# Decoder layer on one core: row normalisations and two bias-free evictions on ScalarE, the maximum's PSUM banks shared, every engine's list reordered

## The reference

```
x = _layernorm(x + attn(x))             # 16 heads of 16, biases, rotary with the row's norm, layernorm of q and k heads, causal
x = _layernorm(x + xattn(x, ctx))       # over the 256 columns: 8 heads of 8, band of 64, relu(o @ w_out.T + b_out) * ctx, w_ct, b_ct
x = _layernorm(x + ffn(x))              # ternary quantised weights, silu(gate) * up (1024 wide), rms_norm, projection

def _layernorm(x, axis=-1, eps=1e-05):
    m = jnp.mean(x, axis=axis, keepdims=True)
    v = jnp.var(x, axis=axis, keepdims=True)
    return (x - m) / jnp.sqrt(v + eps)
```

## Time and profile before

| what | value |
|---|---|
| median of 3 runs | 1081.5 us (1079.98 to 1083.27) |
| the profiled execution's own time | 1079.87 us |
| its span, first to last instruction | 1078.1 us |
| DVE busy | 944.7 us, 88% of the span |
| PE busy | 933.3 us, 87% |
| POOL busy | 816.3 us, 76% |
| ACT busy | 734.7 us, 68% |

### The profile page before, as it was taken

How to read it: one execution, slowest core, us unless ns; L and a number is a source line. 1 busy time by engine, 2 the same in 40 slices (tenths; PEclk the granted TensorE clock), 3 DMA queues, 4 the chain that set the end, 5 groups by cost and what they waited for, 6 DMA issues and landing times.

```text
span 1078.1 us, 26386 instructions
## 1 busy us (share of the span) xinstructions
PE 933.3 (87%) x10449; PEld 547.9 (51%) x10484; DVE 944.7 (88%) x1877; ACT 734.7 (68%) x1203; POOL 816.3 (76%) x1197
## 2 busy tenths in 40 slices
PE   3366688899999999999999999999999999889885
PEld 1133355455555555555555555555555555555453
DVE  3779878899999999999999999999999999988644
ACT  1344356677778777777777777777777777777754
POOL 2764468788988888888889888888888888854542
...
DMA packets 26122, 25.06 MB, mean 23 GB/s; under 512 B 6160, under 2 KB 24976, under 8 KB 26000
## 3 DMA queue, kind: packets, MB, share of 16 engines
...
## 4 chain that ended last, share of the span: by engine, by line
DVE 47%; PE 24%; ACT 12%; POOL 8%; issue 7%; DMA 1%; SPq 1%; POOLq 0%; DVEq 0%
DVE rowmax L1265 12%; POOL prob L1013 5%; DVE hsplit L1322 4%; ACT kT L758 4%; PE ps L420 4%; DVE amax L1209 4%; PE ps L476 3%; PE ps L386 3%; ACT prob_a L764 3%; DVE prob_a L1215 2%; POOL prob L1011 2%; DVE k_rows L1251 2%; DVE q_rows L1251 2%; DVE x L1243 2%; DVE hid L1316 2%
## 5 line engine op out<-in xcount | busy, mean ns | idle before, releaser
L1265 DVE TENSOR_REDUCE rowmax<-ps 128x4 f32<-128x768 f32 x256 | 243.0, 949 | 17.9 <-PE ps L443 17.7
L986 POOL TENSOR_TENSOR hsum<-hsum,minus_half 128x8 f32<-128x8 f32 x128 | 212.4, 1674 | 28.8 <-DVE hsum L1203 28.7
L794 ACT ACTIVATE prob<-ps 128x768 f32<-128x768 f32 x256 | 207.0, 808 | 29.2 <-PE ps L465 29.2
L1011 POOL TENSOR_SCALAR_AFFINE_SELECT prob<-prob 128x256 f32<-128x256 f32 (+1 forms) x256 | 145.9, 570 | 85.2 <-ACT prob L794 85.2
L1013 POOL TENSOR_SCALAR_AFFINE_SELECT prob<-prob 128x512 f32<-128x512 f32 (+1 forms) x256 | 160.7, 628 | 0.0
L782 ACT ACTIVATE high<-ps,bx_col 128x512 f16<-128x512 f32 x128 | 92.5, 773 | 50.8 <-PE ps L420 50.8
L476 PE MATMUL ps<-prob,v_pad 128*32 128x192 f32 x2048 | 111.2, 335 | 10.5 <-POOL prob L1013 10.3
L443 PE MATMUL ps<-k_rows,q_rows 24*128 24x192 f16 x1024 | 87.8, 250 | 4.0 <-DVE rowmax L1265 3.8
L465 PE MATMUL ps<-q_rows,k_rows 26*128 26x192 f16 x1024 | 87.6, 249 | 3.7 <-DMA q_rows<-negmax 2.1
L476 PEld LDWEIGHTS ps<-prob,v_pad 128*32 128x32 f32 x2048 | 53.9, 110 | 70.8 <-issue 43.7
L420 PE MATMUL ps<-x,wx_qk 64*128 64x256 f32 x512 | 77.2, 421 | 11.9 <-DVE hid L1316 9.4
...
## 6 DMA issues: line engine op xcount, KB each, us to landing
...
prob<-in_w_projT ACTq DMA_DIRECT2D x2, 512.0 KB, 12.3
q_rows<-negmax SPq DMA_DIRECT2D x64, 8.0 KB
...
```

The costliest lines, as they stand in the source:

```text
L794: copy(prob[:, 2 * c:2 * c + 2, :, :].rearrange("p u a b -> p u (a b)"), ps[:, STB:STB + 2, 0:2 * QW], ACT.Exp, scale=float(XD) ** -0.5).t ...
L986: last = g.tensor_tensor(hsum[:, 1, h], hsum[:, 0, h], minus_half[:, h], ALU.pow)
L1011: g.affine_select(out=lead, in_=lead, compare_op=ALU.is_ge, fill=0.0, base=BAND - 64 * kb, pattern=[[0, 4], [1, cut]], channel_multiplier=-1)
L1265: v.tensor_reduce(of_head[:, hq:hq + 2, 2 * ng:2 * ng + 2], ps[:, MXB:MXB + 2, 0:2 * QW].rearrange("p j (a b) -> p j a b", a=2), AX, ALU.m ...
```

## The change

- x1, x2, xn and yout are computed by ACT as Identity(rstd * x + nb). DVE only computes nb = -mean * rstd, a column of 128 numbers (`put_xn_nb`, `put_x1_nb`, `put_x2_nb`, `put_yout_nb`).
- v and v_pad are evicted from PSUM by ACT as plain copies, without bias. The bias of v goes through Wo into bo, and that of the column attention's v through w_out into the bias of zr, once, in the setup (`turn_bias`, `carry_bias` on PE, `hold_bias`, `add_bias` on DVE).
- max_lo and row 25 are gone: one DMA instead of two, and st reads 25 rows.
- h_lo is one instruction of 1024 columns. The small rot_eps is now part of x_stats.
- Banks MXB, which held only the maximum's scores, now also hold proj 0 and 2, up 1 and o. New waits come with it: o waits for max 7, proj 0 for attn, mx 0 for rows0, up 1 for max 0, mx 1 for hid1.
- Every list is in another order, and LAST_LAG is 13 instead of 12.

```diff
-LAST_LAG = 12
+LAST_LAG = 13
...
-            def put_v(t):
-                dve.wait_ge(S["v_ps"], t.at(1, 1))
-                v.tensor_tensor(v_own[:, t.buf, :, 0:AD], ps[:, G7, 0:256].rearrange("p (h d) -> p h d", d=AD),
-                                qkv_bias[:, 512:768].rearrange("p (h d) -> p h d", d=AD), ALU.add).then_inc(S["v"], 1)
+            def put_v(t):
+                act.wait_ge(S["v_ps"], t.at(1, 1))
+                copy(v_own[:, t.buf, :, 0:AD], ps[:, G5, 0:256].rearrange("p (h d) -> p h d", d=AD), ACT.Copy).then_inc(S["v"], 1)
...
-            def put_x1(t):
-                dve.wait_ge(S["y1_pow"], t.at(1, 1))
-                v.tensor_scalar(x1[:, t.x1_buf, :], y1[:, :], mv[:, 1, 0:1], rstd[:, 1, 0:1], ALU.subtract, ALU.mult).then_inc(S["x1"], 1)
+            def put_x1_nb(t):
+                dve.wait_ge(S["y1_pow"], t.at(1, 1))
+                v.scalar_tensor_tensor(nb[:, 1, :], mv[:, 1, 0:1], -1.0, rstd[:, 1, :], ALU.mult, ALU.mult)
+            def put_x1(t):
+                copy(x1[:, t.x1_buf, :], y1[:, :], ACT.Identity, bias=nb[:, 1, :], scale=rstd[:, 1, :]).then_inc(S["x1"], 1)
...
+            def turn_bias():
+                pe.wait_ge(s_fold, 1)
+                for i in range(2):
+                    last = tr(ps[:, OTB, 128 * i:128 * i + 128], qkv_bias[:, 512 + 128 * i:640 + 128 * i], ident[:, :])
+                last.then_inc(s_turn, 1)
+            def carry_bias():
+                pe.wait_ge(s_late, 16 * LATE)
+                pe.wait_ge(s_fold, 2)
+                for i in range(2):
+                    mm(ps[:, OTB, 256:512], zr[:, 128 * i:128 * i + 128], wo[:, i, :], start=i == 0, stop=i == 1)
+                mm(ps[:, OTB, 0:1], wx_out[:, :], bx_col[:, 12:13], start=True, stop=True).then_inc(s_turn, 1)
...
             def put_maxrow(t):
-                sp.wait_ge(S["max_lo"], t.at(1, 1))
-                for part in range(2):
-                    sp.dma_start(q_rows[24 + part:128:32, t.buf, :, :], negmax[:, part, :]).then_inc(s_maxrow[t.buf], 16)
+                sp.wait_ge(S["max_hi"], t.at(1, 1))
+                sp.dma_start(q_rows[24:128:32, t.buf, :, :], negmax[:, 0, :]).then_inc(s_maxrow[t.buf], 16)
...
-            def put_h_lo(t, c):
-                if c == 0:
-                    dve.wait_ge(S["h_hi"], t.at(1, 1))
-                h = slice(HID // 2 * c, HID // 2 * c + HID // 2)
-                last = v.scalar_tensor_tensor(hsplit[:, 1, h], hid[:, h], hss[:, 3:4], hsplit[:, 0, h], ALU.mult, ALU.subtract)
+            def put_h_lo1(t):
+                dve.wait_ge(S["h_hi"], t.at(1, 1))
+                v.scalar_tensor_tensor(hsplit[:, 1, :], hid[:, :], hss[:, 3:4], hsplit[:, 0, :], ALU.mult, ALU.subtract).then_inc(S["h_lo1"], 1)
...
-                    last = mm(ps[:, (G6, G5, G6, G5)[c] + n, XT * (c // 2):XT * (c // 2) + XT], wx_qk[q, c, n, :], x1[q, t.x1_buf, :], start=True, stop=True)
+                    last = mm(ps[:, (MXB, G5, MXB, G5)[c] + n, XT * (c // 2):XT * (c // 2) + XT], wx_qk[q, c, n, :], x1[q, t.x1_buf, :], start=True, stop=True)
```

More of the change, by code:

```diff
@@ L325, in put_qk_ps @@
                 pe.wait_ge(S["xnT"], t.at(1, 1))
-                if t.has(6):
-                    pe.wait_ge(S["y2"], t.back(6).at(1, 1))
                 for i in range(2):
@@ L332, in put_v_ps @@
             def put_v_ps(t):
-                if t.has(4):
-                    pe.wait_ge(S["max_lo"], t.back(4).at(1, 1))
+                pe.wait_ge(S["qk"], t.at(1, 1))
                 for i in range(2):
-                    last = mm(ps[:, G7, 0:DIM], xnT[:, i, :], wqkv[:, i, 512:768], start=i == 0, stop=i == 1)
+                    last = mm(ps[:, G5, 0:DIM], xnT[:, i, :], wqkv[:, i, 512:768], start=i == 0, stop=i == 1)
                 last.then_inc(S["v_ps"], 1)
@@ L392, in put_aT_ps @@
                 pe.wait_ge(S["attn"], t.at(1, 1))
+                if t.has(2):
+                    pe.wait_ge(S["max_hi"], t.back(2).at(1, 1))
                 for i in range(2):
-                    last = tr(ps[:, G6, 128 * i:128 * i + 128], attn[:, 128 * i:128 * i + 128], ident[:, :])
+                    last = tr(ps[:, G7, 128 * i:128 * i + 128], attn[:, 128 * i:128 * i + 128], ident[:, :])
                 last.then_inc(S["aT_ps"], 1)
@@ L491, in put_hf_ps, with put_z_ps @@
                 pe.wait_ge(S["heads1"], t.at(1, 1))
+                for i in range(2):
+                    last = tr(ps[:, G6, 128 * i:128 * i + 128], heads[:, i, :], ident[:, :])
+                last.then_inc(S["hf_ps"], 1)
+            def put_z_ps(t):
+                if t.has(-6):
+                    pe.wait_ge(S["qk"], t.back(-6).at(1, 1))
+                pe.wait_ge(S["hf"], t.at(1, 1))
+                if t.has(3):
+                    pe.wait_ge(S["y3"], t.back(3).at(1, 1))
+                mm(ps[:, G5, 0:256], wx_out[:, :], heads_f[:, :, :].rearrange("p a b -> p (a b)"), start=True, stop=True).then_inc(S["z_ps"], 1)
@@ L492, in put_hf_ps, with put_ct_ps @@
+            def put_ct_ps(t):
+                pe.wait_ge(S["gated"], t.at(1, 1))
                 if t.has(2):
                     pe.wait_ge(S["hT0"], t.back(2).at(1, 1))
-                for i in range(2):
-                    last = tr(ps[:, G5, 128 * i:128 * i + 128], heads[:, i, :], ident[:, :])
-                last.then_inc(S["hf_ps"], 1)
-            def put_z_ps(t):
-                pe.wait_ge(S["hf"], t.at(1, 1))
-                if t.has(1):
-                    pe.wait_ge(S["hid0"], t.back(1).at(1, 1))
-                mm(ps[:, G6, 0:256], wx_out[:, :], heads_f[:, :, :].rearrange("p a b -> p (a b)"), start=True, stop=True).then_inc(S["z_ps"], 1)
@@ L841, in put_hT, with put_yout @@
                     act.wait_ge(S["hT_ps1"], t.at(1, 1))
-                copy(hT[:, c, :, :].rearrange("p a b -> p (a b)"), bank16((G5, G7)[c]), ACT.Copy).then_inc(S[f"hT{c}"], 1)
-            def step(at):
-                t = at(-1)
+                copy(hT[:, c, :, :].rearrange("p a b -> p (a b)"), bank16(G6), ACT.Copy).then_inc(S[f"hT{c}"], 1)
+            def put_yout(t):
+                act.wait_ge(S["yout_nb"], t.at(1, 1))
+                if t.has(3):
+                    act.wait_ge(s_out[t.back(3).buf], t.back(3).dma(1))
+                copy(yout[:, t.buf, :], y3[:, :], ACT.Identity, bias=nb[:, 3, :], scale=rstd[:, 3, :]).then_inc(S["yout"], 1)
@@ new lines, in step @@
+                t = at(-9)
+                if t:
+                    put_hid(t, 1)
+                t = at(-5)
+                if t:
+                    put_rows(t, 1)
+                    put_rows(t, 3)
+                    put_max(t, 1)
+                if at.number == 5:
+                    quantise(5, 1)
+                t = at(-7)
+                if t:
+                    put_heads(t, 0)
+                    put_heads(t, 1)
+                t = at(-5)
+                if t:
+                    put_max(t, 2)
```

1050 lines of the change are left out of this document (523 added, 527 removed).

## The result

The changed kernel takes 1021.1 us (median of four runs, 1013.7 to 1024.4) against 1082.0 for the kernel before (1080.0 to 1083.3). The ratio is 0.943, with a 95% interval of 0.937 to 0.949: 5.7% faster. The forecast was 1063 with a range of 1036 to 1091, so it had the direction and missed the size by 42 us.

A forecast was written before the change was run, and what follows sets the result against it. DVE was taken to bound the kernel, PE close behind. Filling 118 + 3, 26 steps of 28.4 us (738.4) and a drain of 201 made 1060.7, plus 1.8 gave 1062.5, said as 1063 us; range 1036 to 1091.

The forecast's parts named there:

- PE. The work is the same: TensorE's busy time per step: same work, three more direct mx/st neighbours save 0.27 us, giving 27.5 us.
- keeps today's 1.3 of short gaps: DVE's list: the 1.3 us a step of short gaps stays, on top of 25.8 us busy.
- 1.3 of new ones: New DVE gaps a step: max 6 0.4, s_max 0.4, and 0.5 for y3 behind down and heads behind tr.
- rival 1: Lists fit better than thought: PE bounds, its waits shrink to 0.3 us, step 27.6, time 1040 us; chance 0.15.
- The filling itself: Time before tile 5 enters: 118 us, 3 us longer because x_stats stands later in its step.
- DVE sets the step: Kernel before: DVE, busy 28.28 of 29.56 us a step, is the bound, with PE 0.55 us behind.
- The rule that additions and multiplications belong on VectorE: Skill rule speaking against moving normalisations to ScalarE: about 0.56 us there against 0.406 on an unhindered DVE.
- the drain, 201: Time after tile 31 enters: 10.3 steps at 19.9 us, 205, less 4 for shorter first steps: 201 us.
- rival 3: The nb products on DVE wait for GpSimd, 1.197 us each; step 31.3 us, time 1143; chance 0.04.
- Rival 2: ScalarE sets the step through waits for late results; slower, for example 29.8 us a step and 1102 us; chance 0.12.
- just fits: ScalarE's dense run, exp 2 to exp 3, 5.6 us, against some 5.6 us of other PE work before st 4.

The follow-up runs named there:

- g1: Changed kernel with scores pieces 0, 1, 4, 5, 6 and 7 computed for the other half of their pair, so all seven mx/st pairs use different array rows; 1008.0 us.
- b1: Kernel before, its lists kept, with only the four normalisations moved from DVE to ScalarE; 1079.0 us, ratio 0.998.
- a1: Changed kernel with the four normalisations put back on DVE in place of their nb products; 1030.7 us, ratio 0.955 to the kernel before.
- b5: b1 with st 7 directly behind mx 0 on PE and its exp ahead of qT and kT on ScalarE; 1079.8 us, ratio 0.999.
- b6: Kernel before, normalisations still on DVE, with st 7 directly behind mx 0 on PE and its exp ahead of qT and kT; 1073.5 us, ratio 0.994.
- d1: Changed kernel with one more Identity on ScalarE, result unused, behind xn in the dense run; 1024.2 us.

## Why the prediction was wrong

The step of 28.4 us was added up on two engines, DVE (25.8 + 1.3 + 1.3) and PE (27.5 + 0.9), and both sums failed.

**The step that failed first: "PE. The work is the same", 27.5.** PE was busy 26.73. The forecast counted three more pairs of mx and st at 0.09 us each, the price of a pair on the same rows of the array, and that was right: the three new pairs are of this kind and worth 0.3. It did not look at tr, pt and val, whose halves now stand next to each other, as neighbours at all: 0.4 us a step. The remaining 0.3 are not attributed. It also passed over the kind of pair that saves more and that the kernel before has too, eight matmuls that start within 0.11 us (553.90 to 554.01 on PE). That did not cost it anything here, but it is what g1 later used. The Trainium skill (TensorE: Matmul & The Clock Gate, Why this matters for your kernels) says that matmuls of few rows in different row groups run at the same time. The trace agrees, and the two may belong to different pieces of the list: mx at 587.81 and st at 587.83.

**The second: "keeps today's 1.3 of short gaps", plus 1.3 of new ones.** DVE is idle 1.56 us a step, not 2.6. Of the new gaps, max 6 has 0.45 (0.4 forecast) and s_max 0.22 (0.4), and the 0.5 behind down and tr did not come; what is left of the old ones and all others is 0.9. So both parts were too large, by 0.6 and 0.4. A gap belongs to a list, and the lists were new. PE's waits, 0.9 forecast, are 0.78 (for attn 0.64, where 0.4 was said). The measured step, 27.51, is by chance next to rival 1's 27.6, which had a chance of 0.15: its waits on PE, 0.3, were 0.78, and PE's work, 27.6 less 0.3, was 26.73, and the two errors nearly cancel. Besides, g1, which takes 0.63 us of PE's work away for 0.17 of step, speaks against PE as the bound. Its time of 1040 was 19 us too long for the reason that follows.

**The third: the first steps were priced as full ones, and the filling was only charged.** The forecast let every step from tile 5 count 28.4. The first five took 130.3 us, not 142: 11.7 us of the 30.4 missed in the steps. The even steps missed the other 18.7, 21 times 0.89. The filling itself was 5.9 shorter than said and the drain 2.4. Why the first steps are so much shorter is open, as said above.

**The reason given for the gain was wrong in part.** "DVE sets the step" held neither before nor after in full: b1 took 0.9 us of DVE's work away for 0.22 of step, and a1 gave 0.62 back for 0.30. By the medians the whole move is worth 9.6 us once the lists are new, against 50 for the rest. The rule that additions and multiplications belong on VectorE (the Trainium skill, ScalarE: Activation LUTs) gave no warning that came true here, but b1 shows the case in which the move is no gain in time, and b5 against b6 one in which it is a loss.

**What was right.** DVE 25.8 (25.95 measured), ACT 24.8 (24.51), the copies 0.383 (0.385 and 0.378), POOL 25.38 (25.42) and its wait for the sum of squares, 1.5 (1.6), and the drain, 201 (198.6). The drain is in part luck: it ran at a granted clock of 0.90, and g1's took 187.2 us at 0.96. `nb` was 0.15 to 0.19 us in the mean and 0.58 at the most, so rival 3 did not come. The Identity took 0.60 to 0.63 and not 0.56; it reads SBUF, where qT reads PSUM, and no run tried whether that is the cause. Rival 2's place was the right one, the dense run of ScalarE is in the chain, but 0.5 us more there cost 0.03 us a step (d1), so that it "just fits" as was said.
